# Second pass over the count matrix of a graph network: the last cell alone, with the rest of the last line stored as zeros at the start of the stage

## What is computed

```
neigh_sum = segment_sum(x[src], dst, num_segments=N)
deg       = segment_sum(ones, dst, num_segments=N)
mean      = neigh_sum / maximum(deg, 1)
```

## Time and profile before

| | us |
|---|---|
| median of 3 runs | 8792.43 |
| lowest, highest run | 8791.13, 8801.91 |
| the profiled execution | 8789.98 |
| its span in the trace | 8788.1 |

### The profile page before, as it was taken

The page is one execution under the profiler, slowest core; times in us unless marked ns, Lnnn a source line. Parts: engine busy times, 40 slices in busy tenths (PEclk is TensorE's granted clock), DMA queues, the critical chain, the costliest instruction groups (busy, mean ns, idle before and its releaser), DMA issues. The chain is left out here.

```text
span 8788.1 us, 152768 instructions
## 1 busy us (share of the span) xinstructions
PE 6369.6 (72%) x40358; PEld 4395.3 (50%) x40359; DVE 4480.7 (51%) x12127; ACT 2215.2 (25%) x4744; POOL 3403.5 (39%) x3460
## 2 busy tenths in 40 slices
PE   0366602666666669999976777767777599959999
PEld 0255501444443335555546767667776355535555
DVE  6877754656666622222227777777777401131111
ACT  1221201333334410100004555435555100000000
POOL 0777776666664100000007777567777000000000
PEclk6678756888898879999989999989999799979999
DMA  0122201222223246676752222222222366636666
GB/s 16 45 71 71 67 3 47 92 85 86 86 93 83 67 124 174 182 186 170 189 135 54 54 55 55 47 57 54 53 55 55 94 191 189 189 87 177 192 191 182
DMA packets 871578, 901.11 MB, mean 103 GB/s; under 512 B 421539, under 2 KB 820226, under 8 KB 864867
## 3 DMA queue, kind: packets, MB, share of 16 engines
q1 hardware_dynamic: 753541, 637.16, 26.4%
q0 software_dynamic: 109664, 179.92, 9.4%
q10 hardware_dynamic: 8064, 80.29, 2.3%
HBM read 722.84 MB, written 93.87 MB: 93 GB/s over the span
## 5 line engine op out<-in xcount | busy, mean ns | idle before, releaser
L1919 POOL DMA_INDIRECT d_row_ring<-table_att,src_at x1664 | 1583.7, 952 | 644.8 <-issue 493.1
L2449 PE MATMUL psum<-e_a_ring,e_parts 128*128 128x448 bf16 x8232 | 1577.5, 353 | 83.6 <-DVE e_parts L2531 83.6
L2449 PEld LDWEIGHTS psum<-e_a_ring,e_parts 128*128 128x128 bf16 x8232 | 806.2, 98 | 824.2 <-issue 87.6
L775 POOL DMA_INDIRECT b_row_ring<-edge_attr,b_entry x896 | 892.3, 996 | 606.3 <-SPq L752 366.2
L794 PE MATMUL psum<-b_hot 128*128 x2920 | 672.6, 373 | 604.9 <-DVE b_hot L976 534.5
L353 POOL DMA_INDIRECT listed<-a_record,a_slot_no x832 | 867.7, 1043 | 315.0 <-issue 272.4
L1327 PE MATMUL psum<-c_a_ring,c_parts 128*128 128x448 bf16 x4116 | 812.8, 356 | 46.3 <-DMA c_a_ring<-adjacency 41.5
L1944 PE MATMUL psum<-edges_out,edges_in 128*128 128x120 f32 x4896 | 694.3, 301 | 157.9 <-ACT edges_in L2010 156.7
L794 PEld LDWEIGHTS psum<-b_hot 128*128 x2920 | 293.2, 100 | 959.0 <-issue 838.5
L1944 PEld LDWEIGHTS psum<-edges_out,edges_in 128*128 128x128 f32 x4896 | 644.0, 212 | 203.7 <-issue 203.7
L976 DVE TENSOR_SCALAR b_hot<-b_iota,b_key_dst 128x896 int16 (+1 forms) x1460 | 710.0, 486 | 2.1 <-issue 2.1
(11 more groups left out here) (427 smaller groups left out, 7939.8 us busy)
## 6 DMA issues: line engine op xcount, KB each, us to landing
e_a_ring<-adjacency SPq DMA_DIRECT2D x1372, 224.0 KB, 2.8
c_a_ring<-adjacency SPq DMA_DIRECT2D x686, 224.0 KB, 2.9
adjacency<-b_line ACTq DMA_DIRECT2D x49, 1568.0 KB
a_cum<-edge_attr SPq DMA_DIRECT2D x103, 512.0 KB
d_row_ring<-table_att,src_at POOLq DMA_INDIRECT x1664
b_row_ring<-edge_attr,b_entry POOLq DMA_INDIRECT x896
listed<-a_record,a_slot_no POOLq DMA_INDIRECT x832
e_a_left<-adjacency_left SPq DMA_DIRECT2D x28, 224.0 KB, 3.3
```

The costliest lines, as they stand in the source:

```text
L775: pool.indirect_dma_start(out=row_ring[:, u % 4, g, 0:D], out_offset=None, in_=a["edge_attr_128"], in_offset=bass.IndirectOffsetOnAxis(ap= ...
L1919: pool.indirect_dma_start(out=row_ring[:, u % 4, g, :], out_offset=None, in_=table_att[layer], in_offset=bass.IndirectOffsetOnAxis(ap=src_ ...
L2449: mm = nc.tensor.matmul(psum[:, 2 * (turn % 2) + v, 0:WIN], parts[:, piece, s, :], a_ring[:, s % SEVEN, v * WIN:(v + 1) * WIN], start=(s = ...
```

## The change

Where no count is heavy, `windows` is now 1 in place of 7, so the second pass makes the last cell alone. `more` is taken from the fours before the last cell. The seven windows of the last line of `adjacency_left` are stored as zeros from `blank` at the start of the block, from ScalarE's queue, as soon as `s_table` is 1. Before the second pass ScalarE waits until the seven stores have landed; the counts of `s_left_out` start 16 x 7 higher. Where a count is heavy, everything is done as before.

```
-                        eng.value_load(left_n[0:1, 1:2], min_val=NWIDE, max_val=NWIDE),
+                        eng.value_load(left_n[0:1, 1:2], min_val=1, max_val=NWIDE),
...
             @blk.scalar
                 act.sem_inc(s_line_out, 16)
                 act.wait_ge(s_table, 1)
+                for w in range(NWIDE):
+                    act.dma_start(adjacency_left[NT - 1, :, w * WIDE:(w + 1) * WIDE], blank[:]).then_inc(s_left_out, 16)
...
+                act.wait_ge(s_left_out, 16 * NWIDE)
                 act.wait_ge(s_left_n, 1)
                 lines, windows, more = left_of(act)
...
-                        hold(act, s_left_out, k * 16 + 16, s_held_act)
+                        hold(act, s_left_out, k * 16 + (16 * NWIDE + 16), s_held_act)
...
             @blk.vector
-                for k, (few, many) in enumerate(((1, NT), (NWIDE, NWIDE), (1, NW // 2))):
+                for k, (few, many) in enumerate(((1, NT), (1, NWIDE), (1, NW // 2))):
...
-                st.by(V.tensor_copy(hit[0:1, 1:2], cell_row[0:1, 2, CELLS - NWIDE:CELLS - NWIDE + 1]))
+                st.by(V.tensor_copy(hit[0:1, 1:2], cell_row[0:1, 2, CELLS - 1:CELLS]))
```

## The result

| | before | changed |
|---|---|---|
| median, us | 8791.78 (4 runs) | 8733.06 (4 runs) |
| lowest, highest | 8787.13, 8801.91 | 8715.79, 8740.12 |
| profiled execution, span | 8789.98, 8788.1 | 8740.12, 8738.4 |
| ratio, 95% interval | | 0.9927 (0.9915 to 0.9940) |

The changed kernel is faster by 0.73% (0.60 to 0.85%). The forecast was 8731.7 us in a range from 8716 to 8748. Two repeats under "Experiments" gave ratios of 0.9930 and 0.9931, with medians 57.2 and 56.4 us under the kernel before on the same chip.

What follows compares the result with a forecast made beforehand. The second pass was taken as a chain with no engine saturated. Saving 60.76 us less 0.1 for register steps, other terms 0, gave 60.7 off the median 8792.43: 8731.7 us, range 8716 to 8748.

Steps and rivals of the forecast that it cites:

- The pass: Second pass at the end of block b: six cells fewer save 60.76 us, bounds 59.7 and 61.0.
- The extra four: Second pass, the one cell left has two fours: its cast comes 2.1 us later, bounds 1.84 and 3.17.
- The register step: Second pass's loop on three engines: one register step more, taken as 0.1 us.
- The wait for the stores: ScalarE before the second pass, waiting for seven zero stores issued some 1650 us earlier: price 0.
- The stores' issue: Start of block b, ScalarE's queue: seven stores take 2.4 to 12.9 us, hidden in 51.84 us of idle time.
- The traffic: Start of block b: 1568 KB of zeros cost 0, bounds 0 and 5.2 us; gathers have 50 us of slack.
- The rival that the stores are in the way: Start of block b: zeros lengthen GpSimd's reduction up to 5.2 us or delay clears up to 12.9; 8736.9 to 8744.6; chance 0.06.
- The 5.81 us ahead of GpSimd's reduction: Start of block b: unexplained time that zeros could lengthen if it were a fetch from memory; term bounds 0 and 5.2 us.
- The clock rival: From block c on, TensorE's clock comes out worse: 1.4% slowdown in block d costs 31 us, giving 8763; chance 0.05.
- One sign of the prediction's last part: From 3135 to the end: forecast wrong if blocks c to e, 5653 us, differ by more than some 15 us.
- the 3064 that was the limit: Start of the second pass: the forecast is wrong if it starts later than 3064.

Runs made afterwards that it cites:

- four-cell kernel: The changed kernel with four cells in the second pass in place of one; median 8758.05 us (6 runs), ratio 0.9966 to the kernel before.
- stores alone: The kernel before plus the seven zero stores and ScalarE's wait, second pass still seven cells; median 8793.49 us (10 runs), ratio 1.0003.
- five lines: The changed kernel with zeros stored for five lines in place of one (35 stores, 7840 KB); median 8728.63 us (4 runs), ratio 0.9935 to the kernel before.

## Why the prediction was right

*The pass.* The two events give 71.25 - 11.04 = 60.21 us in the first profile; means over three profiles of the kernel before and four of the changed one give 70.96 - 10.45 = 60.5 us. The sum was 60.7. The extra four was priced well within its bounds: 16 matmuls took 5.42 us where 5.24 was taken, and 4.49 to 4.86 in the three repeats. In the pass the granted clock was 0.66 in the first profile and 0.83 to 0.84 in those. That the median came out within 1.4 us of the forecast is luck in part: its four runs lie between 8715.79 and 8740.12.

*The register step* was the one mis-sized term. I took 0.1 us for all engines together. The rows of the four-cell kernel show 0.36 us more between cast and clear in the first turn, 0.11 later, and one-four cells some 0.25 us longer (10.39 against 10.10 to 10.16). The changed kernel's only turn is a first one (2.64 against 2.27 us). So it was about 0.4 us and not 0.1. I put it down to the register steps, since they are what the change adds to the loop; no run shows them alone.

*The wait for the stores* cost nothing: ScalarE was idle for 12.55 us before the cast, and stores issued right there cost 1.2 us.

*The stores' issue* came out between the two rows that I had as bounds, near the lower: 3.48 us for seven, 0.48 each in the median (the earlier trace rows give 0.34). The upper bound was misread: of the 14 loads in the earlier trace rows SyncE issued seven in 5.3 us, 0.76 us each, and then waited for TensorE to free slots of `a_ring` (L1176), so 1.85 us each is no price of an issue. By that row seven stores cost at most 5.3 us, not 12.9. ScalarE's gap before the first cell covers 21.5 us as well.

*The traffic* is also as forecast. The rival that the stores are in the way has nothing for it in the kernel with the stores alone, nor with five times the bytes. The rule of the Trainium skill ("DMA: Bandwidth & Descriptors", "Issuing engines are not separate DMA queues") is that transfers of different issuing engines interleave on the same 16 DMA engines. With five lines both queues did use them in one stretch (last section). Whether the gathers landed later for it is not recorded; TensorE's need came 50 us later in either case and hid it if they did, as the prediction had it. The 5.81 us ahead of GpSimd's reduction stayed 5.8 to 6.1 us, with or without stores.

*The clock rival* was right as a spread, and not as a loss of 31 us or more. The changed kernel's block d halves were at 0.94 and 0.93 in its first profile, before at 0.97 and 0.93:

```profile
4634.00:5624.00 990.00, 769.56 (x6815) 702.14 (x6814) 761.21 (x2411) 516.24 (x1562) 718.10 (x760) 0.94 0.24 54
5734.00:6724.00 990.00, 773.87 (x6741) 710.60 (x6740) 753.23 (x2385) 511.58 (x1547) 723.01 (x765) 0.93 0.24 54
```

6815 matmuls in place of 6866 is 0.7% fewer, in the first half, and block d was 13.6 us longer. One sign of the prediction's last part came up by that: blocks c to e differed by 16.4 us, over the 15 that I allowed. I had sized one execution's scatter by the runs' total, in which the blocks' scatters partly cancel. The pass began at 3058.4, earlier than the 3064 that was the limit, and so the cast to `high` and the start of block c came at 3063.92 and 3069.41 and not near 3069.7 and 3074.8: nothing in the sum allowed for a first pass that ends 5.8 us earlier by itself.

Against this rival I had read from two halves of block d that its pace hardly followed the clock. The 13 profiles say that it follows it in part: 35.9 us more of busy TensorE go with 16.2 us of length, the shortest block against the longest. That the clock is the cause is still argued and not shown, since no run here sets it; and whether the change has a part in it stays open, as said above.

## What to carry to other kernels

A stretch in which every engine waits for the next one costs its whole length. Find it by windows with low busy shares everywhere, price it by the distance between equal events, and expect to get back the cells that are cut. Work whose result is known before can be stored ahead, on a queue whose engine has a long gap before its next work; measure that gap first. Then look at who reads the result: a line of zeros was cheap to make, but multiplying with it 42 times, and loading it once transposed, cost another 54 to 57 us until that was skipped too. And compare a change of 60 us by the stretch that it touches, since two profiles of one program can differ by 10 us or more in each of two long stretches.

## What the runs showed of the hardware that I had not expected

GpSimd's first gather instructions of the block took 1.72 to 2.46 us whether the DMA engines were nearly idle (share 0.10 from 1414 to 1424 in the kernel before) or full with ScalarE's stores (35 stores, 30 of the 40 slices below at 80% or more); so contention does not explain their slowness:

```profile
DMA  0000039999999999999999988999999999993300
...
q10 hardware_dynamic: 5040, 8.03, 73.1%
q0 software_dynamic: 224, 0.46, 5.2%
```

These are the DMA shares in 40 slices of the stretch from 1400 to 1430 in the kernel with five lines, and its two queues, ScalarE's and GpSimd's.

In the first pass, the profiles of one and the same work part ways early. Counted from the first cast of a cell, the stores of the lines are level within 1.1 us up to about 1573 us, and by about 1677 us four profiles (the changed kernel, its repeat, stores alone, five lines) are 4 to 8 us ahead of the other five that I compared. One of the four still does seven cells in its second pass, so this is not the change. In the 18 us at the parting (from 1570 and from 1569) the kernel before was granted 0.86 of the clock and did 50 matmuls, the changed kernel 0.91 and 72; which was the cause of which is not shown. Afterwards the lead changes only slowly: at the store of the last line the changed kernel is 5.7 us ahead of the profile before, its repeat 14.3 us.
